# Joining the expert combination and the linear attention of a gated decoder into one stage of four blocks

## The reference, cut to what matters

```python
x = x + tanh(g_ffn[1])   * L1_ffn(layernorm(x))             # each token: its expert's row
x = x + tanh(g_xattn[2]) * L2_xattn(layernorm(x), ctx, ctx, mask)

def L2_xattn(q, k, v, mask):            # 16 heads of 16
    Q, K, V = heads(q @ wq.T + bq), heads(k @ wk.T + bk), heads(v @ wv.T + bv)
    attn = where(mask, -inf, Q @ K.T / dk)
    o = (attn @ V) @ wo.T + bo
    return ln_g * normalise(q + o) + ln_b
```

## Time and profile before

| | us |
|---|---|
| median of three runs | 1611.55 |
| lowest and highest | 1608.13, 1616.25 |
| the profiled execution | 1616.99 |
| its span, first to last instruction | 1615.0 |
| TensorE's mean granted clock | 0.928 |

### The profile page before, as it was taken

One profiled execution on the slowest core, in us unless ns is written; L12 is line 12 of the kernel. 1 busy time (PEld: TensorE's weight loads), 2 busy tenths in 40 slices (PEclk: granted clock), 3 DMA queues, 4 the chain that ended last, 5 costly groups with the idle time before them and its releaser, 6 DMA issues. The chain is left out here.

```text
span 1615.0 us, 29206 instructions
## 1 busy us (share of the span) xinstructions
PE 1413.2 (88%) x9657; PEld 1137.9 (70%) x9658; DVE 699.5 (43%) x2244; ACT 654.9 (41%) x1469; POOL 490.8 (30%) x556
## 2 busy tenths in 40 slices
PE   5999979999999999699997899957587898777598
PEld 3666756799999986467775789955366777545487
DVE  4666725200000006267762500035753564558575
ACT  3354533244444442146563244433334444323352
POOL 4356530122222210223322022215327633121330
PEclk9799988999999999779998999977799999888799
DMA  8500006366665633000002755630036874010000
GB/s 279 158 2 1 2 1 215 119 208 195 202 206 190 207 128 104 0 1 2 1 2 67 237 162 201 205 102 1 0 150 211 274 221 142 1 52 1 1 26 26
DMA packets 111951, 173.75 MB, mean 108 GB/s; under 512 B 20427, under 2 KB 88669, under 8 KB 111337
## 3 DMA queue, kind: packets, MB, share of 16 engines
q1 hardware_dynamic: 101679, 144.26, 28.0%
q0 software_dynamic: 10176, 28.24, 4.9%
HBM read 133.06 MB, written 39.35 MB: 107 GB/s over the span
## 5 line engine op out<-in xcount | busy, mean ns | idle before, releaser
L1416 ACT ACTIVATE kT<-ps,b_sb 128x128 f32<-128x128 f32 x312 | 114.6, 367 | 155.9 <-PE ps L1525 134.8
L704 ACT ACTIVATE wbuf<-ps 128x512 f32<-128x512 f32 (+1 forms) x256 | 123.3, 543 | 87.4 <-PE ps L942 86.9
L1525 PEld LDWEIGHTS ps<-qT,wbuf 128*128 128x128 f32 x1248 | 145.4, 192 | 3.9 <-issue 1.9
L1525 PE MATMUL ps<-qT,wbuf 128*128 128x128 f32 x1248 | 145.7, 275 | 1.7 <-issue 1.7
L1535 PE MATMUL ps<-L0f_second,kT 128*128 x624 | 141.1, 379 | 0.0
L274 POOL TENSOR_TENSOR sm<-sm,mhalf 128x4 f32<-128x4 f32 (+1 forms) x40 | 45.0, 1125 | 294.7 <-DVE sm L269 294.7
L1535 PEld LDWEIGHTS ps<-L0f_second,kT 128*128 128x128 f32 x624 | 115.6, 190 | 14.1
L942 PE MATMUL ps<-nmT_r,sel_r 32*128 32x256 f32 (+1 forms) x512 | 109.6, 427 | 0.0
L747 DVE CUSTOM_DVE_ANT_0 ps<-ps,ts 128x128 f32<-128x128 f32 (+1 forms) x256 | 83.1, 389 | 46.4 <-PE ps L918 46.4
L750 DVE TENSOR_REDUCE nmax<-ps 128x2 f32<-128x512 f32 x128 | 80.3, 682 | 49.2 <-PE ps L918 49.1
L352 ACT ACTIVATE xnT<-ps 128x512 f32<-128x512 f32 x64 | 36.4, 595 | 131.8 <-PE ps L329 62.9
(11 more groups left out here) (444 smaller groups left out, 3184.8 us busy)
## 6 DMA issues: line engine op xcount, KB each, us to landing
wbuf<-in_L_w SPq DMA_DIRECT2D x66, 1024.0 KB, 9.9
tree_rows<-rt SPq DMA_DIRECT2D x3, 3151.0 KB, 23.1
prob<-tree_rows SPq DMA_DIRECT2D x69, 137.0 KB
tree_outputs<-probT SPq DMA_DIRECT2D x69, 128.0 KB
L0f_second<-in_L_w SPq DMA_DIRECT2D x8, 1024.0 KB, 11.6
ts<-in_L_b SPq DMA_DIRECT2D x58, 128.0 KB, 2.9
wbuf<-in_L_rec SPq DMA_DIRECT2D x3, 2048.0 KB, 10.5
expert_rows<-vbuf SPq DMA_DIRECT2D x2, 2048.0 KB, 10.3
```

The source lines that it names most:

```text
L704: act.activation(PT[:, k, :, q0:], ps[:, a_bank("ST", b, k), :].rearrange("p (h s) -> p h s", h=2)[:, :, q0:], ACT.Exp, scale=scale).then_ ...
L1416: act.activation(hs[:, f, :], hidden(f), func, bias=b1_sb[:, v, f:f + 1]).then_inc(h_in, 1)
L1525: ins = pe.matmul(hidden(f), first[v][:, kk, f * P:(f + 1) * P], xgT[:, kk, :], start=(kk == 0), stop=(kk == KD - 1))
```

## The change

Combining, first norm and its transposes leave the expert stage and become the head of each block in the attention stage. The expert stage now ends when the last expert row is stored. In the attention, `combine` stands in VectorE's queue behind the mask's reduction; the norm that feeds the attention is a third pair, `first`, with room of its own in `stats` and `sm`; `kv` moves from `probT` to a part of `wbuf`, as `probT` now receives the loaded rows; `add_rows` waits for `first`'s rows, and its bias half becomes `add_bias` with a semaphore of its own. Transposes into the attention ("in") and out of it ("out") share two PSUM banks in the order in0, in1, in2, out0, in3, out1, out2, out3. The core of the diff:

```diff
@@ phase_resident: VectorE, SyncE, GpSimd, ScalarE, TensorE
-                    for blk in range(NB):
-                        combine(blk)
-                    for blk in range(NB):
-                        load_result(blk)
-                    for blk in range(NB):
-                        nrm[blk % 2].power(pool, blk // 2, 0)
-                    result(0)
-                    for blk in range(NB):
-                        if blk + 1 < NB:
-                            result(blk + 1)
-                        norm_T(blk)
@@ phase_linear
-            kv = [probT[:, blk] for blk in range(NB)]
+            kv = [wbuf[:, 1, blk * 512:(blk + 1) * 512].rearrange("p (a d) -> p a d", a=2) for blk in range(NB)]
...
+            first = [Norm(n + f"first{i}", 1, 4, 16 + 4 * i, on_act=True) for i in range(2)]
...
+                    for blk in range(NB):
+                        rows = a["yg"][blk * BLK:(blk + 1) * BLK]
+                        sp.dma_start(gat[blk], rows.rearrange("(t p) d -> p t d", p=P)).then_inc(got[blk], 16)
@@ GpSimd
                     def add_rows(blk):
                         tiles = slice(blk * 4, blk * 4 + 4)
+                        pool.wait_ge(first[blk % 2].link, first[blk % 2].done(blk // 2, 0))
...
                     own_heads(0)
+                    own_heads(1)
+                    power(first, 0)
+                    power(first, 1)
                     pool.wait_ge(scaled, 1)
                     add_rows(0)
+                    add_bias(0)
+                    power(post, 0)
+                    power(first, 2)
                     add_rows(1)
+                    power(post, 1)
+                    own_heads(2)
+                    power(nrm, 0)
+                    add_bias(1)
+                    power(first, 3)
+                    add_rows(2)
+                    own_heads(3)
+                    power(post, 2)
+                    add_bias(2)
+                    power(nrm, 1)
+                    add_rows(3)
+                    power(post, 3)
+                    add_bias(3)
+                    power(nrm, 2)
+                    power(nrm, 3)
@@ ScalarE
+                    rows_in(0)
                     for blk in range(NB):
+                        if blk + 1 < NB:
+                            rows_in(blk + 1)
+                        turned("in", blk)
                         for m in range(KD):
                             act.wait_ge(q_full, blk * 2 + (m + 1))
...
                         if blk >= 2:
-                            turned(blk - 2)
+                            rows_out(blk - 2)
+                            turned("out", blk - 2)
@@ VectorE
+                    combine(0)
+                    combine(1)
                     outputs(0)
                     for blk in range(NB):
+                        if blk + 2 < NB:
+                            combine(blk + 2)
                         if blk + 1 < NB:
                             outputs(blk + 1)
                         residual(blk)
@@ TensorE
                     for blk in range(NB):
+                        turn_in(blk)
+                        pe.wait_ge(xT_in, turn_no("in", blk, 1) + 1)
                         for m in range(KD):
...
```

More of the change, by code:

```diff
@@ L1801, in ring_step @@
                         dve.tensor_tensor(y_sb[v], ps[:, 4 + v, 0:D], b2_sb[:, v, :], ALU.add).then_inc(y_out[v], 1)
[L1803 to L1812, removed]
                     dve.wait_ge(ld_rowsA, 48)
@@ L2018, in ring_step @@
                         ins.then_inc(y_full[v], 1)
[L2020 to L2030, removed]
                     pe.wait_ge(ld_att[0], 32)
@@ L2077, in phase_linear, with turn_no @@
             xb = wbuf[:, 0].rearrange("p (t d) -> p t d", t=NT)
+            turns = [turn for blk in range(NB) for turn in (("in", blk), ("out", blk - 2))] + [("out", NB - 2), ("out", NB - 1)]
+            turns = [turn for turn in turns if turn[1] >= 0]
+            def turn_no(kind, blk, u):
+                return 2 * turns.index((kind, blk)) + u
             def x_of(blk):
@@ L2099, in _, with power @@
+                    def power(norms, blk):
+                        norms[blk % 2].power(pool, blk // 2, 0)
                     own_heads(0)
+                    own_heads(1)
+                    power(first, 0)
+                    power(first, 1)
                     pool.wait_ge(scaled, 1)
                     add_rows(0)
-                    own_heads(1)
+                    add_bias(0)
+                    power(post, 0)
+                    power(first, 2)
                     add_rows(1)
[L2104 to L2110, removed]
@@ L2113, in _, with result, rows_in @@
+                    power(nrm, 2)
+                    power(nrm, 3)
                 @block.scalar
                 def _(act):
-                    def turned(blk):
-                        nrm[blk % 2].result_on_act(act, blk // 2, 0, lambda t: xs4[blk % 2][:, t, :], x_of(blk))
+                    def result(norms, outs, blk):
+                        norms[blk % 2].result_on_act(act, blk // 2, 0, outs, x_of(blk))
+                    def rows_in(blk):
+                        result(first, lambda t: xn_tok[:, blk * 4 + t, :], blk)
@@ L2129, in _ @@
                         if blk >= 2:
-                            turned(blk - 2)
-                    turned(NB - 2)
-                    turned(NB - 1)
+                            rows_out(blk - 2)
+                            turned("out", blk - 2)
+                    for blk in range(NB - 2, NB):
+                        rows_out(blk)
+                        turned("out", blk)
                 @block.vector
@@ L2146, in _, with combine @@
                     dve.wait_ge(scaled, 1)
+                    def combine(blk):
+                        own = first[blk % 2]
+                        dve.wait_ge(got[blk], 16)
+                        for t in range(4):
+                            i = blk * 4 + t
+                            ins = dve.scalar_tensor_tensor(x_tok[:, i, :], gat[blk][:, t, :], gate(gi), x_tok[:, i, :], ALU.mult, ALU.add)
+                        ins.then_inc(added, 1)
+                        dve.wait_ge(added, blk + 1)
+                        if blk >= 2:
+                            dve.wait_ge(own.link, own.done(blk // 2 - 1, 0))
+                        own.statistics(dve, blk // 2, 0, x_of(blk))
                     def outputs(blk):
                         ts = ts4[blk % 2]
-                        dve.wait_ge(pre, blk * 2 + 1)
+                        dve.wait_ge(pre, blk + 1)
                         for u in range(2):
@@ L2177, in _, with turn, turn_in, turn_out @@
                 def _(pe):
-                    def turn(blk):
-                        pe.wait_ge(nrm[blk % 2].link, nrm[blk % 2].done(blk // 2, 0))
+                    def turn(kind, norms, rows, blk):
+                        pe.wait_ge(norms[blk % 2].link, norms[blk % 2].done(blk // 2, 0))
                         for u in range(2):
-                            wait(pe, xT_in, (blk - 1) * 2 + u + 1)
-                            transpose_pair(pe, 7 - u, xs4[blk % 2][:, 2 * u:2 * u + 2, :]).then_inc(n_full, 1)
+                            no = turn_no(kind, blk, u)
+                            wait(pe, xT_in, no - 1)
+                            transpose_pair(pe, 6 + no % 2, rows[:, 2 * u:2 * u + 2, :]).then_inc(n_full, 1)
+                    def turn_in(blk):
+                        turn("in", first, xn_tok[:, blk * 4:blk * 4 + 4, :], blk)
+                    def turn_out(blk):
+                        turn("out", nrm, xs4[blk % 2], blk)
                     pe.wait_ge(ld_att[0], 32)
                     for blk in range(NB):
+                        turn_in(blk)
+                        pe.wait_ge(xT_in, turn_no("in", blk, 1) + 1)
                         for m in range(KD):
@@ L2206, in _ @@
                         if blk >= 2:
[L2207 to L2209 removed]
+                            turn_out(blk - 2)
+                    turn_out(NB - 2)
+                    turn_out(NB - 1)
         class Single:
```

47 lines of the change are left out of this document (19 added, 28 removed).

## The result

| | median us | lowest and highest | profiled execution | its span | mean granted clock |
|---|---|---|---|---|---|
| before | 1612.21 (4 runs) | 1608.13, 1616.25 | 1616.99 | 1615.0 | 0.928 |
| changed | 1643.51 (4 runs) | 1641.21, 1646.20 | 1645.76 | 1643.8 | 0.926 |

The changed kernel is slower: ratio 1.0189, 95% interval 1.0169 to 1.0209, 31.3 us by the medians. The profiled executions put the loss in the joined stage: from the first load of the experts' rows to the first transfer of the tree stage the kernel before takes 97.96 us (1073.68 to 1171.64) and the changed one 126.93, 29.0 more, and the profiled executions differ by 28.8.

The account below looks back on a forecast made before the run. The target was the serial 27.0 us ahead of the attention's barrier. Entry, links, slower blocks 1 and 2 and a longer end pay 61.7 us for 27.0 gained: 1611.55 + 34.6 = 1646 us, range 1631 to 1654.

Parts of the forecast that it names:

- entry, to Q(0): From the stage's start to block 0's first q matmul, through loads, scaling, combine, norm and copies: 20.6 us.
- block 0: First attention block, from its q products to the end of its output product: 13.0 us, as before the change.
- link 0 to 1: TensorE's new wait between block 0's output product and block 1's q, through outputs(0), combine(2), power, rows_in(2), copies: 12.4 us.
- block 1: Second attention block, starting at low clock after TensorE's idle time: 12.3 us, the mean of two slow blocks.
- link 1 to 2: Wait between block 1's output product and block 2's q, with residual(0), combine(3) and GpSimd collisions: 20.3 us.
- block 2: Third attention block, booked slower by 2.5 us than at full clock, like the block ahead of it.
- end, from O(2): From block 2's output product to the last transposed copy, mostly VectorE's outputs and residuals: 39.8 us instead of 36.4.
- Collisions: GpSimd's long adds slowing VectorE's operations beside them: 2.1, 2.35 and 2.35 us booked; 4.7 more possible.
- Clock: TensorE's low clock at the start of blocks 1 and 2: 2.5 us each; unknown from -4.6 to +1.5.
- Bare chain: Rival: waits in order are real, but no collisions cost and the clock recovers early: +23.2 us, 1634.8; chance 0.12.
- Third rival (powers lock too): Rival: six GpSimd powers each hold up VectorE's products by a full 1.18 us: +41.7 us, 1653.2; chance 0.05.
- The overlap pays: Rival: statistics are ready early, no block waits, VectorE's work alone sets the end: -8.9 us, 1602.6; chance 0.04.

Follow-up runs that it names:

- e3: Changed kernel with VectorE's four combines ahead of outputs(0) and GpSimd's own_heads and first-norm powers moved early to match; 1616.37 us, ratio 1.0008 to the kernel before.
- e8: As e7, with the scaling of the rows and the mask's reduction moved into the expert stage ahead of its ring; 1593.25 us, ratio 0.9882 to the kernel before.
- e1: Changed kernel with ScalarE writing block b's normalised rows directly ahead of its copies of block b; 1621.54 us, ratio 1.0039 to the kernel before.
- e5: Changed kernel with 11 and 19 unread products on TensorE in the gaps ahead of blocks 1 and 2; 1640.59 us, ratio 1.0171 to the kernel before.
- e7: Changed kernel's work with four queues reordered: all combines first, outputs and residuals in turn, powers early; 1598.97 us, ratio 0.9914 to the kernel before.
- e4: Changed kernel with 22 and 38 unread products on TensorE in the gaps ahead of blocks 1 and 2; 1663.12 us, ratio 1.0312 to the kernel before.
- e2: Changed kernel with VectorE combining all four blocks ahead of outputs(0), other queues unchanged; 1643.40 us, ratio 1.0182 to the kernel before.
- e6: Changed kernel with GpSimd's four add_bias cut to one column of each tile, queue orders unchanged; 1640.66 us, ratio 1.0168 to the kernel before.
- e9: Kernel before, barrier kept, with outputs(b) and residual(b) in turn on VectorE and GpSimd's norm power behind post's; 1610.12 us, ratio 0.9986 to the kernel before.

## Why the prediction was right, point by point

The forecast of +34.6 us met +31.3 by the medians (1643.51 against a forecast of 1646) and +29.7 at the last transposed copy (1199.89 + 0.60 = 1200.49 against 1170.82). All terms lie where they were put, each but block 1 a little smaller:

| term | forecast | measured |
|---|---|---|
| start of the stage | 1074.67 | 1074.46 |
| entry, to Q(0) | 20.6 | 19.0 |
| block 0 | 13.0 | 12.8 |
| link 0 to 1 | 12.4 | 11.9 |
| block 1 | 12.3 | 12.5 |
| link 1 to 2 | 20.3 | 19.3 |
| block 2 | 12.3 | 12.0 |
| end, from O(2) | 39.8 | 38.5 |

- **Entry.** I let the scaling wait for both own_heads. It took 1.53 us again although GpSimd's two took 2.66 (and e3's four 5.11), and 0.48 in e8 with none beside it: it was held up by the first at most. And both small steps behind the reduction took 0.17 and 0.18, where 0.40 and 1.19 stood before; I had credited one of them. combine(0) came 6.37 us after the start, not 7.5.
- **Links.** The chain was as written: combine behind outputs, power, rows_in, copies. e1 and e3 show that it held only with both of its ends: with either one cut, the links shrink to 1.6 us.
- **Collisions.** Booked with 6.8 us, measured 5.5: own_heads(2) cost 0.9 (four products in 2.55 instead of 1.67), add_bias(1) 0.7, add_bias(2) and (3) 2.0 each, less than an add's 2.35, since the add had begun 0.4 us ahead of the products that it held up.
- **Clock.** Blocks 1 and 2 took 12.5 and 12.0 us, around the 12.3 that was the mean of the two slow blocks, and e5 shows that the clock made it.
- **Bare chain** fell: both discounts that it took, no collisions and an early clock, were wrong, by 5.5 and 4.3 us.
- **Third rival (powers lock too).** It fell: VectorE's four products beside a power of 1.18 us took 1.67 in the changed kernel (1134.01), close to the 1.66 in the earlier trace rows. The four took 2.55 us beside own_heads(2) (1.46) and 3.64 beside add_bias(2) (2.53).
- **"The overlap pays"** fell at the point that was named: VectorE was free for 15.7 us before O(0) and could not use it, because outputs(0) stood first. e7 puts the combines there. That rival's 1161.9 for the last copy was too high even so: with the orders free (e7) it comes at some 1152.
- **Slips that cost nothing.** The stage's first matmul did not come 27 us earlier: it is now block 0's transposes, at 1088.85 against 1101.70. The stage as a whole did start that early. And the upper end of the range doesn't follow from its terms: 1652.4 and a spread of 3.4 give 1655.8, not 1654.

Between the profiled executions and the medians 2.5 us remain (+28.8 and +31.3), and single runs of one kernel differ by 5 us and more (1641.2 to 1646.2 for the changed one).

The eleven traces show where part of that lies. From the first transfer of the tree stage to the end, where all kernels have the same instructions, the profiled executions take 438.6 to 443.4 us: 438.6 in e8, 438.8 in e4, 439.3 in e2, and 442.2 to 443.4 in the others. The tree stage (to the load of in_pad) took 175.4 to 180.3, and the stretch behind it (to the next weights) 64.5 to 69.1; in the first 20 us of that stretch the granted clock was 0.83 in the kernel before and 1.00 in the changed one. Block 0's q products vary as well, from 5.11 to 6.72 us.

So it is partly luck that the profiled executions' +28.8 matches the stage's +29.0: outside the stage the changed kernel was 0.8 later at its start and lost 3.2 in the tree stage, but won 4.6 in the stretch behind it. What decides these steps, and whether the order of one stage moves the clock of a later one, stays open.

## What to carry to other kernels

When a barrier is replaced by a pipeline, write down for each engine's queue what stands ahead of the step that the next block needs, and follow it through all queues: here three orders written one block ahead made a circle that lengthened the stage by 29 us, and the same work in another order made it 19 us shorter than before the change. An engine's idle time ahead of a wait was of use only to what its queue had in front of that wait (VectorE's 15.7 us ahead of outputs(0)). Cutting the circle in one queue may only hand the wait to the next (e2); cut it where the chain is fed (e3) or where it is consumed (e1), and look at the trace again. A gain of 3 to 5 us in one stage can hide in what the other stages do from run to run (e2, e5, e6): read it from the stage's own rows.

## What the runs showed of the hardware

- A float32 product of 128x128 on 512 columns took 0.86 us at clock 1.00 and is two records in the rows (e4: 19.05 us for 22).
- After gaps of 11.05 and 18.41 us, the eight records of a block's q products took 6.09 and 5.58 us instead of 3.60 to 3.70, at a granted clock of 0.80 and 0.84 over the block; with other products in the gap they took 3.70 each time, at 1.00 (e5).
- With the same instructions ahead of them, block 0's q products took 6.52 us in the changed kernel, 6.39 in e4, 6.41 in e6 and 5.40 in e5, and 6.72 and 5.69 in the kernel before and in e9: the same start from clock 0.50 costs up to 1.1 us more or less from one execution to another.
- A four-element step of VectorE with both inputs in SBUF waited for the whole rest of a GpSimd add (0.90 us in the changed kernel and 1.84 in the kernel before instead of 0.17; it ended at 1144.68 and 1138.59 where the add ended at 1144.66 and 1138.58), while VectorE's bn_stats, with one input, ran beside the changed kernel's add_bias(1) at its usual 1.06 us for three.
